# Expert stage of an attention-plus-MoE block: weight loads tied to scatter landings, gathers further ahead, deeper result buffers, one buffer for silu and product

## The chip, the cores and the metric

The kernel runs on 1 core of one Trainium2 chip. The metric is device time in microseconds (us), from start to end of one launch. Engines: TensorE (PE, with its weight loads as PEld), VectorE (DVE), ScalarE (ACT), GpSimd (POOL), and SyncE (SP), which here only issues DMAs. SP's DMAs run in queue q1, POOL's indirect DMAs in queue q0; both are carried by the same 16 DMA engines.

## What is computed

One transformer block over 2048 tokens of width 512, in float32: linear attention (16 heads of 128), then a mixture of experts. Its last part, which the change touches, is

```python
gu = jnp.einsum('ech,ehf->ecf', buf, w_gate_up)      # 32 experts, 512 -> 2 x 256
g, u = jnp.split(gu, 2, axis=-1)
act = jax.nn.silu(g) * u
y = jnp.einsum('eci,eih->ech', act, w_down)          # 256 -> 512
routed_out = jnp.einsum('tk,tkh->th', w_r, y_exp)    # weighted sum over a token's experts
```

`buf[e]` are the layer-normed rows of the tokens that chose expert e (at most 256 in two tiles of 128); each row carries its routing weights behind it, so that `act` can be multiplied by the weight before the second product. The result is added to the residual already in `out`.

## The kernel before

Attention and routing come first and fill some 730 us. Then `experts` runs 32 experts (NE), one after the other. Each needs 1 MB of up weights (two DMAs of 512 KB) and 512 KB of down weights; every float32 matrix is split into a high and a low part (ACT copies to fp32r, DVE subtracts), so each product is three rounds of matmuls.

For expert e, tile t (0 or 1; the second only for experts with enough tokens, decided at run time by `both`):

- POOL, `gather` (L1213): an indirect DMA brings the token rows into `xg[:, e % 6, t]`; six slots. From e = 6 it waits for `m_a` of expert e-5 by count, that is for the product of expert e-6, the last reader of the slot.
- PE, `turn` (L1254): transposes into PX; ACT `x_high` (L1378) and DVE `x_low` (L1324) split it.
- PE, `up` (L1268): 12 matmuls into PG. ACT `silu` (L1401) writes `s`, DVE `act` (L1331) multiplies with the other half of PG and the weight into `a[:, e % 2, t]`.
- PE, `turn_a` (L1277), ACT `a_high`, DVE `a_low`, PE `down` (L1290): 6 matmuls into PY.
- ACT, `weigh` (L1413): copies PY to `y[:, e % 4, t]`. From e = 4 it waits until the scatters of expert e-4 have landed (`m_s`, 32 counts an expert).
- POOL, `scatter` (L1223): an indirect DMA adds the rows of `y` to `out`. The first of an expert waits until all scatters of the expert before have landed, since two may hit the same row. Experts whose row count is above 64 get two scatters, the others one of 64 rows.

The order on each engine is written by hand. PE in iteration e does `turn_a(e-1)`, `turn(e+1)`, `up(e)`, `down(e-1)`; ACT and DVE split the weights of expert e+2 in iteration e, and `weigh(e-1)` is ACT's last there. POOL in iteration e gathers expert e+6 and then scatters expert e, after twelve gathers ahead of the loop.

SP loads weights into a ring of eight experts. `load e` (e from 8 on) waits for `up(e-8)` and `down(e-8)`, and also for `m_wl`, the count of low parts that DVE has made: part p of load e may start when part p of expert e-5 has been split, which DVE does in iteration e-7.

In the text, iteration e of an engine is its loop body for e; "expert k's scatter" is the one of L1223 for k. In the trace the two-scatter experts are 0, 1, 11, 15, 18, 25 and 27, and PE works two tiles for 0, 1, 11, 18, 25 and 27.

Of the kernel before, what the change touches and what calls it, by code (L numbers as in the profile page):

```python
# [5 lines left out]
P = 128  # L6
D = 512
# [5 lines left out]
NE = 32  # L13
# [8 lines left out]
ALU = mybir.AluOpType  # L22
ACT = mybir.ActivationFunctionType
# [1054 lines left out]
RING = 8  # L1078

def load_up(sm, eng, ring, wgu, e, halves=(0, 1)):
    up, _, _, _ = ring[e % RING]
    for i in halves:
        k = slice(2 * i, 2 * i + 2)
        eng.dma_start(up[:, k, :], wgu[e, k].rearrange("k p f -> p k f")).then_inc(sm[f"m_wg{e % RING}"], 16)

def load_down(sm, eng, ring, wd, e):
    _, down, _, _ = ring[e % RING]
    eng.dma_start(down, wd[e].rearrange("k p f -> p k f")).then_inc(sm[f"m_wd{e % RING}"], 16)  # L1090
# [32 lines left out]
def experts(nc, sm, wgu, wd, xn2d, out, si, ring, consts, w_h, w_l, v_h):  # L1123

    with ExitStack() as ctx:
        def sb(name, shape, dt=F32):
            return ctx.enter_context(nc.sbuf_tensor("m_" + name, shape, dt))

        def ps(name, n=512):  # L1130
            return ctx.enter_context(nc.psum_tensor("m_" + name, [P, n], F32))

        xg = sb("xg", [P, 6, 2, XW])
        xT_h = sb("xT_h", [P, 2, 2, 4, P], F32R)
        xT_l = sb("xT_l", [P, 2, 2, 4, P], F32R)
        s = sb("s", [P, 2, 256])
        a = sb("a", [P, 2, 2, 256])
        a_h = sb("a_h", [P, 2, 256], F32R)
        a_l = sb("a_l", [P, 2, 256], F32R)
        y = sb("y", [P, 4, 2, D])  # L1140
        with nc.sbuf_tensor("m_raw", [P, 2, 512], F32) as raw:
            pass
        low = sb("low", [P, 2, 512], F32R)
# [4 lines left out]
        PG = [ps("PG0"), ps("PG1")]  # L1148
        PA = [ps("PA0"), ps("PA1")]
        PY = [ps("PY0"), ps("PY1")]  # L1150
# [9 lines left out]
        def flags(eng, name):  # L1160
            return [eng.alloc_register(f"{name}{i}") for i in range(7)]
# [20 lines left out]
        with nc.Block() as block:  # L1182
            @block.sync
            def _(eng):
                eng.dma_start(ident[:, :], consts[:, 0:128]).then_inc(sm["m_id"], 16)
                eng.wait_ge(sm["m_g01"], 16)
                load_up(sm, eng, ring, wgu, 6)
                load_down(sm, eng, ring, wd, 6)
                eng.wait_ge(sm["m_g11"], 16)
                load_down(sm, eng, ring, wd, 7)  # L1190
                for e in range(RING, NE):
                    for part in range(3):
                        for t in range(2):
                            eng.wait_ge(sm[f"m_gu{t}" if part < 2 else f"m_yd{t}"], e - RING + 1)
                        eng.wait_ge(sm["m_wl"], 3 * (e - RING + 3) + part + 1)
                        if part < 2:
                            load_up(sm, eng, ring, wgu, e, (part,))
                        else:
                            load_down(sm, eng, ring, wd, e)
                eng.wait_ge(sm["m_s"], 32 * NE)  # L1200

            @block.gpsimd
            def _(eng):
                regs = flags(eng, "mp")

                def gather(e, t):

                    i = 2 * e + t
                    if e >= 6:
                        eng.wait_ge(sm[f"m_a{t}"], e - 5)  # L1210
                    else:
                        eng.wait_ge(sm["m_xg"], i + 1)
                    eng.indirect_dma_start(  # L1213
                        xg[:, e % 6, t, :], None, xn2d[:, :],
                        bass.IndirectOffsetOnAxis(ap=si[:, i:i + 1], axis=0),
                        bounds_check=T - 1, oob_is_err=False).then_inc(sm[f"m_g{t}{e % 6}"], 16)

                def scatter(e, t, rows, done):
                    i = 2 * e + t
                    if t == 0 and e >= 1:  # L1220
                        eng.wait_ge(sm["m_s"], 32 * e)
                    eng.wait_ge(sm[f"m_y{t}"], e + 1)  # L1222
                    eng.indirect_dma_start(  # L1223
                        out[:, :], bass.IndirectOffsetOnAxis(ap=si[0:rows, i:i + 1], axis=0),
                        y[0:rows, e % 4, t, :], None, compute_op=ALU.add).then_inc(sm["m_s"], done)

                for e in range(6):
                    gather(e, 0)
                    gather(e, 1)
                for e in range(NE):  # L1230
                    if e + 6 < NE:
                        gather(e + 6, 0)
                        gather(e + 6, 1)
                    if e == 0:
                        eng.wait_ge(sm["m_full"], 1)
                    load_full(eng, regs, e)
                    with eng.If_lt(regs[e % 7], T):  # L1237
                        scatter(e, 0, P, 16)
                        scatter(e, 1, P, 16)
                    with eng.Else():  # L1240
                        scatter(e, 0, 64, 32)
# [71 lines left out]
            @block.vector  # L1313
            def _(eng):
                regs = flags(eng, "mv")

                def w_low(e, parts):
                    if e < NE:
                        for part in parts:
                            split_low(sm, eng, ring, w_h, e, part)  # L1320

                def x_low(e, t):
                    eng.wait_ge(sm[f"m_xTh{t}"], e + 1)
                    eng.tensor_tensor(flat(xT_l[:, e % 2, t]), PX[t][:, :], f(flat(xT_h[:, e % 2, t])),  # L1324
                                             ALU.subtract).then_inc(sm[f"m_xTl{t}"], 1)

                def act(e, t):
                    eng.wait_ge(sm[f"m_si{t}"], e + 1)
                    if e >= 2:
                        eng.wait_ge(sm[f"m_at{t}"], e - 1)  # L1330
                    eng.scalar_tensor_tensor(out=a[:, e % 2, t, :], in0=PG[t][:, 256:512],  # L1331
                                             scalar=xg[:, e % 6, t, D + e:D + e + 1], in1=s[:, t, :],
                                             op0=ALU.mult, op1=ALU.mult).then_inc(sm[f"m_a{t}"], 1)

                def a_low(e, t):
                    eng.wait_ge(sm[f"m_ah{t}"], e + 1)
                    eng.tensor_tensor(a_l[:, t, :], PA[t][:, 0:256], f(a_h[:, t, :]), ALU.subtract).then_inc(sm[f"m_al{t}"], 1)

                def clear(e, t):
                    eng.memset(xg[:, e, t, :], 0.0).then_inc(sm["m_xg"], 1)  # L1340

                for e in range(4):
                    clear(e, 0)
                    clear(e, 1)
                load_flag(eng, regs, 0)
                both(eng, regs, 0, x_low, "m_xTl1")
                for e in range(4, 6):
                    clear(e, 0)
                    clear(e, 1)
                eng.tensor_copy(full[:, :], si[64:65, :]).then_inc(sm["m_full"], 1)  # L1350
                w_low(0, (2,))
                w_low(1, (0,))
                load_flag(eng, regs, 1)
                both(eng, regs, 0, act, "m_a1")
                w_low(1, (1,))
                both(eng, regs, 1, x_low, "m_xTl1")
                both(eng, regs, 0, a_low, "m_al1")
                w_low(1, (2,))
                w_low(2, (0, 1))
                load_flag(eng, regs, 2)  # L1360
                both(eng, regs, 2, x_low, "m_xTl1")
                w_low(2, (2,))
                both(eng, regs, 1, act, "m_a1")
                w_low(3, (0, 1, 2))
                for e in range(2, NE + 1):
                    load_flag(eng, regs, e + 1)
                    both(eng, regs, e - 1, a_low, "m_al1")
                    both(eng, regs, e + 1, x_low, "m_xTl1")
                    w_low(e + 2, (0, 1))
                    both(eng, regs, e, act, "m_a1")  # L1370
                    w_low(e + 2, (2,))

            @block.scalar
            def _(eng):
# [21 lines left out]

                def silu(e, t):
                    eng.wait_ge(sm[f"m_gu{t}"], e + 1)
                    if e >= 1:
                        eng.wait_ge(sm[f"m_a{t}"], e)  # L1400
                    eng.activation(s[:, t, :], PG[t][:, 0:256], ACT.Silu).then_inc(sm[f"m_si{t}"], 1)  # L1401

                def a_high(e, t):
                    eng.wait_ge(sm[f"m_at{t}"], e + 1)
# [3 lines left out]

                def weigh(e, t):
                    eng.wait_ge(sm[f"m_yd{t}"], e + 1)  # L1410
                    if e >= 4:
                        eng.wait_ge(sm["m_s"], 32 * (e - 3))
                    eng.activation(y[:, e % 4, t, :], PY[t][:, :], ACT.Copy).then_inc(sm[f"m_y{t}"], 1)  # L1413

                w_high(1, (0, 1))
                eng.wait_ge(sm["m_id"], 16)
# [90 lines left out]
```

## Time and profile before

| | |
|---|---|
| time, median of 3 runs | 973.87 us (973.5 to 981.56) |
| the profiled execution's time | 979.09 us |
| its span in the trace | 977.3 us |
| busy in the span: PE / DVE / ACT / POOL | 92% / 79% / 51% / 49% |
| first transpose of the expert stage | 740.1 us |
| last matmul of the expert stage ends | 962.5 us |
| last scatter starts | 969.2 us |

Times in the trace are counted from the start of the span. A row of the timeline gives start, duration, engine, line and operation, how many were merged, and in brackets the idle time before it with what ended it. A row of the windows gives busy time and count for each engine, then the granted TensorE clock (1.00 is full), the mean busy share of the 16 DMA engines and the GB/s moved.

### The profile page before, as it was taken

How to read it: one execution, taken by the hardware profiler on the slowest of the kernel's cores; microseconds unless marked ns; L12 is line 12 of the kernel's file. 1: busy time of each engine (PE TensorE's matmuls, PEld its weight loads, DVE VectorE, ACT ScalarE, POOL GpSimd, SP SyncE). 2: the span in 40 equal slices, each digit the busy share in tenths (PEclk: the TensorE clock that was granted, in tenths of full speed). 3: DMA queues.
4: the chain of work that ended last, by engine and by line, in shares of the span. 5: the costliest groups of instructions: out<-in, count | busy, mean ns of one | idle time of the engine just before them, and what ended most of it. 6: DMA issues, size and time to landing. Idle time of an engine off the chain costs nothing. (4 is left out here: it accounts for less than half of the span.)

```text
span 977.3 us, 14567 instructions
## 1 busy us (share of the span) xinstructions
PE 902.5 (92%) x4362; PEld 731.1 (75%) x4362; DVE 772.9 (79%) x1843; ACT 503.3 (51%) x867; POOL 482.5 (49%) x395
## 2 busy tenths in 40 slices
PE   4789999999999999999969999999976999998893
PEld 3577888888888888888848888888854677776672
DVE  6978888888888889888977777777776788887670
ACT  5455655555554655554563222332224687876671
POOL 2466766666766667766630000000006456775662
PEclk9999999999999999999999999999998999999897
DMA  8001111111111111110563676443155699999633
GB/s 309 6 33 49 51 46 50 59 45 49 39 59 50 44 59 51 39 59 35 195 224 145 209 266 208 148 148 119 56 192 185 162 331 323 293 299 279 201 43 43
DMA packets 67368, 127.06 MB, mean 130 GB/s; under 512 B 12072, under 2 KB 14504, under 8 KB 65232
## 3 DMA queue, kind: packets, MB, share of 16 engines
q1 hardware_dynamic: 58144, 114.67, 33.7%
q0 software_dynamic: 9136, 11.31, 6.2%
q8 instruction: 43, 0.70, 0.3%
q14 instruction: 45, 0.37, 0.1%
HBM read 106.53 MB, written 32.90 MB: 143 GB/s over the span
## 5 line engine op out<-in xcount | busy, mean ns | idle before, releaser
L595 POOL TENSOR_TENSOR a_t<-a_t 128x512 f32<-128x512 f32 x80 | 105.1, 1314 | 99.0 <-DVE a_t L358 99.0
L604 POOL TENSOR_TENSOR a_fQ<-a_fQ,a_den 128x512 f32<-128x512 f32 x64 | 88.0, 1375 | 71.8 <-DVE a_den L396 71.8
L213 PE MATMUL a_PQ<-w_h,a_xT_h 128*128 128x512 f32 x384 | 106.9, 400 | 10.1 <-DVE w_l L345 9.4
L782 PE MATMUL r_PY<-w_h,r_o_h 128*128 128x512 f32 x256 | 105.9, 414 | 3.4 <-DVE r_o_l L884 3.4
L1070 POOL TENSOR_SCALAR r_vr<-r_mv 128x1 f32<-128x1 f32 x16 | 8.4, 525 | 196.6 <-DVE r_mv L895 196.6
L213 PE MATMUL a_PQ<-w_l,a_xT_h 128*128 128x512 f32 x384 | 104.5, 395 | 0.0
L213 PE MATMUL a_PQ<-w_h,a_xT_l 128*128 128x512 f32 x384 | 103.4, 391 | 0.0
L782 PE MATMUL r_PY<-w_h,r_o_l 128*128 128x512 f32 x256 | 101.0, 395 | 0.0
L1223 POOL DMA_INDIRECT out<-m_y,si x39 | 69.1, 1772 | 64.5 <-DMA out<-m_y,si 51.2
L782 PE MATMUL r_PY<-w_l,r_o_h 128*128 128x512 f32 x256 | 100.5, 393 | 0.0
L392 DVE CUSTOM_DVE_ANT_0 a_m<-a_fQ,a_z 128x128 f32<-128x128 f32 x256 | 100.4, 445 | 0.0
L1213 POOL DMA_INDIRECT m_xg<-xn2d,si x64 | 79.0, 1235 | 39.5 <-DVE m_xg L1340 18.2
L611 POOL TENSOR_TENSOR a_A_l<-a_A,a_A_h 128x512 fp32r<-128x512 f32 x64 | 89.0, 1391 | 6.5 <-ACT a_A_h L480 6.5
L213 PEld LDWEIGHTS a_PQ<-w_h,a_xT_h 128*128 128x128 f32 x384 | 70.0, 190 | 25.3 <-issue 11.2
L357 DVE TENSOR_TENSOR a_t<-a_PQ,a_tab 128x512 f32<-128x512 f32 x80 | 55.0, 688 | 41.7 <-PE a_PQ L213 41.7
L213 PEld LDWEIGHTS a_PQ<-w_l,a_xT_h 128*128 128x128 f32 x384 | 73.2, 191 | 15.8
L494 ACT ACTIVATE a_t<-a_t 128x512 f32<-128x512 f32 x80 | 50.0, 625 | 67.4 <-POOL a_t L595 67.2
L213 PEld LDWEIGHTS a_PQ<-w_h,a_xT_l 128*128 128x128 f32 x384 | 72.9, 190 | 15.4
L480 ACT ACTIVATE a_QT_h<-a_PT 128x512 fp32r<-128x512 f32 x64 | 38.1, 596 | 80.7 <-PE a_PT L221 80.7
L1120 DVE TENSOR_TENSOR w_l<-v_l,w_h 128x1024 fp32r<-128x1024 f32 x48 | 57.2, 1222 | 5.7 <-ACT w_h L1114 4.3
L782 PEld LDWEIGHTS r_PY<-w_h,r_o_h 128*128 128x128 f32 x256 | 48.5, 189 | 12.0 <-issue 3.8
L782 PEld LDWEIGHTS r_PY<-w_h,r_o_l 128*128 128x128 f32 x256 | 48.5, 189 | 11.2
(182 smaller groups left out, 2245.3 us busy)
## 6 DMA issues: line engine op xcount, KB each, us to landing
oT<-a_o SPq DMA_DIRECT2D x64, 256.0 KB, 2.4
v_l<-in_wgu SPq DMA_DIRECT2D x32, 512.0 KB
raw<-in_wgu SPq DMA_DIRECT2D x24, 512.0 KB
v_l<-oT SPq DMA_DIRECT2D x11, 1024.0 KB, 7.2
v_l<-in_wd SPq DMA_DIRECT2D x16, 512.0 KB
raw<-in_wd SPq DMA_DIRECT2D x12, 512.0 KB
v_h<-oT SPq DMA_DIRECT2D x5, 1024.0 KB, 6.9
out<-r_x SPq DMA_DIRECT2D x18, 256.0 KB, 2.0
```

What stands on the lines that cost most here:

```text
L213: last = eng.matmul(bank[:, :], a[:, k, :], w[:, 4 * i + k, :], start=s == 0 and k == 0, stop=s == 2 and k == 3)
L357: eng.tensor_tensor(heads(t1[:, r % 2, :]), q, spread(tab[:, c % 2, 0, :]), ALU.mult)
L392: last = eng.tensor_tensor_reduce(m[:, cols], fQ[:, n % 3, cols], z[:, c % 2, g * P:(g + 1) * P], 1.0, 1e-6, ALU.mult, ALU.add, den[:, n % ...
L480: eng.activation(out, in_, ACT.Copy).then_inc(sm[kind], 1)
L494: eng.activation(t2[:, r % 2, :], t1[:, r % 2, :], ACT.Relu, scale=-1.0).then_inc(sm["r"], 1)
L595: eng.tensor_tensor(t1[:, r % 2, :], t1[:, r % 2, :], t2[:, r % 2, :], ALU.add).then_inc(sm["xr"], 1)
L604: eng.tensor_tensor(q, q, den[:, n % 2, :].unsqueeze(2).broadcast_to([P, 4, P]), ALU.mult).then_inc(sm["fs"], 1)
L611: eng.tensor_tensor(A_l[:, n % 2, :], A[:, n % 2, :], f(A_h[:, n % 2, :]), ALU.subtract).then_inc(sm["Al"], 1)
L782: last = eng.matmul(PY[c % 2][:, :], a[:, c % 2, h * P:(h + 1) * P], b[:, h, :], start=h == 0 and s == 0, stop=h == NH - 1 and s == 2)
L1120: eng.tensor_tensor(low, src, high.bitcast(F32), ALU.subtract).then_inc(sm["m_wl"], 1)
L1213: eng.indirect_dma_start(xg[:, e % 6, t, :], None, xn2d[:, :], bass.IndirectOffsetOnAxis(ap=si[:, i:i + 1], axis=0), bounds_check=T - 1, o ...
L1223: eng.indirect_dma_start(out[:, :], bass.IndirectOffsetOnAxis(ap=si[0:rows, i:i + 1], axis=0), y[0:rows, e % 4, t, :], None, compute_op=AL ...
```

## The change

Five edits, all in `experts`:

1. The load of expert e no longer waits for DVE's split; from e = 10 it waits for the landed scatters of expert e-10 (count 32(e-9)). Loads 8 and 9 wait only for `up` and `down` of experts 0 and 1.
2. POOL gathers further ahead: in its iteration e up to expert e+6 for e < 3, e+7 for e from 3, e+8 from 8. The number of slots stays six.
3. `y` becomes two buffers: six results for first tiles, four for second tiles; `weigh` waits for the scatters of expert e-6 or e-4.
4. `silu` writes into `a`, and the product overwrites it; `s` is gone. `silu` now waits for `turn_a(e-2)` where it waited for the product of e-1, and `act` loses its own wait.
5. In SBUF `y` grows from 16 to 20 KB a partition and `s` (2 KB) goes.

```diff
-        s = sb("s", [P, 2, 256])
-        y = sb("y", [P, 4, 2, D])
+        y = [sb("y0", [P, 6, D]), sb("y1", [P, 4, D])]
+        deep = (6, 4)
@@ SP
-                        eng.wait_ge(sm["m_wl"], 3 * (e - RING + 3) + part + 1)
+                        if e >= RING + 2:
+                            eng.wait_ge(sm["m_s"], 32 * (e - RING - 1))
@@ POOL, scatter
-                        y[0:rows, e % 4, t, :], None, compute_op=ALU.add).then_inc(sm["m_s"], done)
+                        y[t][0:rows, e % deep[t], :], None, compute_op=ALU.add).then_inc(sm["m_s"], done)
@@ POOL
+                asked = 6
                 for e in range(NE):
-                    if e + 6 < NE:
-                        gather(e + 6, 0)
-                        gather(e + 6, 1)
+                    ahead = e + 7 + (e >= 3) + (e >= 8)
+                    while asked < min(ahead, NE):
+                        gather(asked, 0)
+                        gather(asked, 1)
+                        asked += 1
@@ DVE, act
-                    if e >= 2:
-                        eng.wait_ge(sm[f"m_at{t}"], e - 1)
                     eng.scalar_tensor_tensor(out=a[:, e % 2, t, :], in0=PG[t][:, 256:512],
-                                             scalar=xg[:, e % 6, t, D + e:D + e + 1], in1=s[:, t, :],
+                                             scalar=xg[:, e % 6, t, D + e:D + e + 1], in1=a[:, e % 2, t, :],
@@ ACT, silu
-                    if e >= 1:
-                        eng.wait_ge(sm[f"m_a{t}"], e)
-                    eng.activation(s[:, t, :], PG[t][:, 0:256], ACT.Silu).then_inc(sm[f"m_si{t}"], 1)
+                    if e >= 2:
+                        eng.wait_ge(sm[f"m_at{t}"], e - 1)
+                    eng.activation(a[:, e % 2, t, :], PG[t][:, 0:256], ACT.Silu).then_inc(sm[f"m_si{t}"], 1)
@@ ACT, weigh
-                    if e >= 4:
-                        eng.wait_ge(sm["m_s"], 32 * (e - 3))
-                    eng.activation(y[:, e % 4, t, :], PY[t][:, :], ACT.Copy).then_inc(sm[f"m_y{t}"], 1)
+                    if e >= deep[t]:
+                        eng.wait_ge(sm["m_s"], 32 * (e - deep[t] + 1))
+                    eng.activation(y[t][:, e % deep[t], :], PY[t][:, :], ACT.Copy).then_inc(sm[f"m_y{t}"], 1)
```

## Rows read from the trace of the kernel before

**Rows 1.** Chain that ended last: start, us, what; the link through a gather
```profile
902.42 6.56 DMA m_xg<-xn2d,si
```

**Rows 2.** Groups by line, POOL, 784 to 917 us
```profile
L1213 POOL DMA_INDIRECT m_xg<-xn2d,si x38 | 49.7, 1307 | 11.6 <-issue 11.0 <-ACT m_y L1413 0.3 <-DVE m_a L1331 0.3
L1223 POOL DMA_INDIRECT out<-m_y,si x23 | 42.5, 1847 | 33.5 <-DMA out<-m_y,si 31.7 <-issue 1.2 <-ACTq L1180 0.6
```

**Rows 3.** Timeline of POOL: scatters (experts 1, 2, 3, 8, 10, 11, 15, 21, 24, 25, 30, 31)
```profile
776.33 1.57 POOL L1223 DMA_INDIRECT out<-m_y,si  x1 [0.30 <-issue]
...
784.95 1.67 POOL L1223 DMA_INDIRECT out<-m_y,si  x1 [4.12 <-DMA out<-m_y,si]
...
791.76 1.98 POOL L1223 DMA_INDIRECT out<-m_y,si  x1 [2.48 <-DMA out<-m_y,si]
...
824.06 2.29 POOL L1223 DMA_INDIRECT out<-m_y,si  x1 [0.91 <-DMA out<-m_y,si]
...
837.18 2.14 POOL L1223 DMA_INDIRECT out<-m_y,si  x1 [0.30 <-issue]
...
843.16 1.94 POOL L1223 DMA_INDIRECT out<-m_y,si  x1 [0.30 <-issue]
...
871.37 2.20 POOL L1223 DMA_INDIRECT out<-m_y,si  x1 [0.74 <-DMA out<-m_y,si]
...
916.63 1.48 POOL L1223 DMA_INDIRECT out<-m_y,si  x1 [0.30 <-issue]
...
933.31 1.93 POOL L1223 DMA_INDIRECT out<-m_y,si  x1 [0.31 <-issue]
...
938.19 2.06 POOL L1223 DMA_INDIRECT out<-m_y,si  x1 [0.31 <-issue]
...
965.34 1.44 POOL L1223 DMA_INDIRECT out<-m_y,si  x1 [2.52 <-DMA out<-m_y,si]
969.18 1.43 POOL L1223 DMA_INDIRECT out<-m_y,si  x1 [2.40 <-DMA out<-m_y,si]
```

**Rows 4.** Timeline of PE: starts of iterations 21, 22, 25; late transposes; the last matmuls
```profile
882.85 0.44 PE L1277 MATMUL m_PA<-m_ident,m_a 128*128 128x128 f32 x2 [0.94 <-DVE m_a L1331]
...
888.42 0.44 PE L1277 MATMUL m_PA<-m_ident,m_a 128*128 128x128 f32 x2
...
907.14 1.11 PE L1254 MATMUL m_PX<-m_ident,m_xg 128*128 128x128 f32 x4 [3.95 <-DMA m_xg<-xn2d,si]
...
915.26 0.38 PE L1277 MATMUL m_PA<-m_ident,m_a 128*128 128x128 f32 x2
...
961.88 0.62 PE L1290 MATMUL m_PY<-w_h,m_a_l 128*128 128x512 f32 x2
```

**Rows 5.** Timeline of SP's queue: up loads of experts 8, 12 and 31
```profile
768.41 1.50 SPq L1085 DMA_DIRECT2D raw<-in_wgu  x2
...
789.79 1.50 SPq L1085 DMA_DIRECT2D v_l<-in_wgu  x2
...
913.07 1.50 SPq L1085 DMA_DIRECT2D v_h<-in_wgu  x2
```

**Rows 6.** Windows, all engines, columns as told above
```profile
784.00:917.00 133.00, 120.82 (x549) 92.39 (x549) 106.13 (x133) 102.34 (x155) 91.04 (x61) 0.96 0.95 299
748.00:768.00 20.00, 14.20 (x61) 10.79 (x60) 11.38 (x16) 9.41 (x16) 10.77 (x9) 0.83 0.36 78
785.00:790.00 5.00, 4.77 (x23) 3.48 (x22) 4.39 (x7) 4.25 (x7) 3.67 (x3) 1.00 1.06 386
830.00:835.00 5.00, 5.00 (x27) 4.20 (x26) 4.41 (x5) 4.20 (x7) 3.57 (x2) 1.00 0.74 229
```

**Rows 7.** Windows at the start of the stage, and ACT's late silu in the timeline
```profile
747.50:750.00 2.50, 1.60 (x12) 1.12 (x10) 1.11 (x2) 0.00 (x0) 1.89 (x3) 1.00 1.05 386
...
750.00:752.50 2.50, 0.37 (x2) 0.29 (x2) 0.91 (x2) 0.38 (x1) 1.89 (x3) 0.92 0.21 55
...
751.17 0.38 ACT L1401 ACTIVATE m_s<-m_PG 128x256 f32<-128x256 f32 x1 [5.59 <-remote]
```

## Prediction

> **What bounds the kernel now.** I read the chain that ended last first, then POOL's groups by line, then the timelines of POOL, PE and SP, then windows. The chain names POOL's scatters and gathers from 897 us on, with one detour through a gather that landed late and the transposes behind it [rows 1]. So the question is how long POOL has been the limit. Its groups between 784 and 917 us add up to the stretch: gathers 49.7 + 11.6 us, scatters 42.5 + 33.5 us, together 137 us with the edges, and of the idle part 31.7 us ended when an earlier scatter landed [rows 2]. Only traces of idle time ended on a result or on a free gather slot (0.3 us each). POOL never waits for PE there; it is a chain of its own, gather, gather, scatter, wait for the landing, from expert 1's second scatter at 776.33 to expert 31's at 969.18 [rows 3].
>
> Its pace is the next thing to see. From expert 3's scatter (791.76) to expert 21's (916.63) are 124.9 us for 18 experts. Three of these (11, 15, 18) have a second scatter, which costs an issue of 1.85 + 0.3 us [rows 2], 6.5 us together, so one expert takes (124.9 - 6.5) / 18 = 6.58 us. PE's iteration takes 5.57 us (882.85 to 888.42) [rows 4]. POOL falls behind a microsecond an expert, until PE meets it: expert 25's gather, issued by 902.42, lands 6.56 us later [rows 1] and PE's transposes wait 3.95 us for it [rows 4]. Between iteration starts 888.42 and 915.26 PE takes 26.84 us for three iterations that need 3 x 5.57 + 0.4 (a second transpose tile) = 17.1, so it loses 9.8 us, part of it as slower matmuls after the idle time. That loss isn't the end's cause: even after it the end hangs on POOL, whose last scatter starts 6.7 us after the last matmul has ended (961.88 + 0.62) [rows 3, 4].
>
> Why 6.58 us? The DMA engines are 95% busy from 784 to 917 us at 299 GB/s, 386 GB/s at the best of these windows [rows 6]. Where their share fell to 0.74, at 830 to 835, the following scatters came 5.98 us apart (837.18 to 843.16), with no wait for a landing [rows 3, 6]. Once the loads are over, the distance is 4.88 us with gathers (933.31 to 938.19) and 3.84 us without (965.34 to 969.18) [rows 3].
>
> **Loads tied to landings.** Per POOL iteration the weights are the same amount: landing k releases load k+10, and before, between scatters 3 and 21, loads 13 to 31 went out too. What changes is when. Before, PE's and DVE's pace of 5.6 us pushes loads at a POOL that takes 6.58; now a load follows POOL's own landings, so the queue is less deep on average, and the idle gap after a PE stall is not followed by a crowd. Bounds for the pace: unchanged at 6.58, and 5.07 us, what POOL needs if every wait for a landing went ((133 - 31.7) / 20 experts) [rows 2]. The nearest row is 5.98 at a lighter load [rows 3]; but the new load is issued at the very moment when the next scatter is, so I don't take all of it: 6.2 us, 0.38 x 18 = **-6.8 us** (0 to -27).
>
> The first loads move too. Load 8 waited for DVE until 768.41 [rows 5]; it now starts when `up(0)` is done, about 748, and load 9's up part about 765. The DMA engines are 36% busy from 748 to 768 [rows 6], so some 1.5 to 2.5 MB leave the crowded stretch. Expert 2's scatter waited 4.12 us and expert 3's 2.48 us for landings [rows 3]; 2 MB at 386 GB/s is 5 us of DMA time. I take half of that two-step wait, **-3 us** (0 to -5).
>
> Are the later loads late? Load 31 goes out when scatter 21 has landed, about 922 at the old pace against 913.07 [rows 5], and its first reader is ACT's split in iteration 29, three iterations of 5.57 us and the last products before the end of PE's work: about 944, or 934 with PE unstalled. A load takes 1.57 MB / 299 GB/s = 5.3 us. That leaves over 6 us even then, so the price is nothing, as long as POOL's lag stays under about six iterations.
>
> **Code fetch at the start.** While loads 6 and 7 saturate DMA (share 1.05 to 750 us), ACT stands for 5.59 us for something outside its program and resumes at 751.17, just as the share drops to 0.21 [rows 7]. Load 8's 1.05 MB now comes right behind and prolongs the crowd by 1.05 / 386 = 2.7 us. If ACT's fetch sits behind it, PE and with it POOL's first scatters come that much later; 0 to +2.7, I take **+1.5 us**. By that rule the price would be the full 2.7 and the sum 1.2 us worse; the trace agrees that the wait ends with the crowd, but shows no second case.
>
> **Gathers further ahead.** Same 64 gathers. In POOL's iterations 3 and 8 four are issued instead of two: 2 x (1.31 + 0.3) = 3.2 us each [rows 2], of which the waits for a landing there hid 2.48 and 0.91 [rows 3]: +0.7 and +2.3. Iterations 24 and 25 lose theirs: at most 4.88 - 3.84 = 1.04 us for each [rows 3], together I take -1.6. Net **+1.4 us** (-1 to +5). The gather of expert e+8 must wait for the product of expert e+2, with scatter e queued behind it on POOL. POOL works expert 21's scatter at 916.63, when PE is in iteration 25: the product is there. Around experts 9 to 11 the lead is near two iterations and it may cost 1 us, inside that bound. On PE's side the two iterations of lead (11 us) cover the 6.56 us of a late gather: the 9.8 us stall goes. It isn't in the sum, since the end hangs on POOL; it says what PE would allow.
>
> **Six results.** `weigh` waits for scatter e-6 where it was e-4. It only matters where POOL is more than four iterations behind, which is so where scatter 21 starts at 916.63 with PE already in its iteration 25 (915.26) [rows 3, 4]; it removes the same stall as the gathers, again off POOL's chain: 0. Second tiles keep four; experts 18, 25, 27 need scatters 14, 21, 23, landed before by the pace above.
>
> **Silu and product in one buffer.** Same instructions and sizes; the new wait (a transpose of two experts ago) is long over when `up` ends, DVE has one instruction less: 0 to -1 us over 32 experts, on PE and so covered.
>
> **Sum.** -6.8 - 3 + 1.5 + 1.4 = -6.9 us on the profiled execution: 979.1 - 6.9 = 972.2. That execution was 5.2 us over the median of 973.87; by the median it would be 967.0. Its stalls and POOL's lag seem part of that difference, so most of the effect should be there in a median run: **968 us**.
>
> **Rivals.**
> - *PE becomes the limit.* If POOL's pace falls to about 5.9, the chain no longer binds. PE ends 9.8 us sooner, and the last scatter starts 1 us behind it instead of 6.7: -15.5, so 958.4 by the median and 963.6 by the profile, 961. For: POOL's waits hold 31.7 us. Against: POOL's issues alone went to 5.98 us where no landing was waited for. Chance 0.22.
> - *POOL's pace stays.* Equal bytes between equal scatters, equal landing time. Then only the small terms are left, about 0: 973 to 976. For: DMA share 0.95. The Trainium skill, "DMA: Bandwidth & Descriptors", section "Queues, rings and completion order", says that each DMA engine takes turns between queue rows packet by packet; by that a deep load queue would not hold a scatter back more than a shallow one, and pacing loads gives nothing. Expert 15's scatter at 871.37 had waited only 0.74 us for a landing in the loaded stretch [rows 3], which fits it in part; expert 2's 4.12 us doesn't. Chance 0.23.
> - *Slower: the burst meets the scatter.* Each landing releases 1.5 MB of loads and the next scatter at once. If that makes every landing as slow as the worst rows (784.95 to 791.76, 6.8 us; 7.1 with a little more), POOL takes +0.4 to 0.5 us an expert, +8 over 18, and the extra gathers come on top: 980 to 984. It decides from a pace of 6.7 us. Chance 0.15.
> - *As forecast*, pace 6.0 to 6.4: 963 to 972. Chance 0.40.
>
> About 1% (9.7 us) is what a measurement of this kernel can tell from no change. Faster by more (under 964.1) takes the first rival and a small part of the forecast: 0.30. Slower by more (over 983.6) only the top of the third: 0.10. The rest, 0.60, is the same. The range reaches from the first rival's 959 to 979, leaving out its best part and most of the slower case.
>
> **What would show it.** Right: scatters 3 to 21 about 6.2 us apart with less wait on `out` landings; no PE wait for `m_xg`; load 8 issued about 748 and load 31 after scatter 21; the last scatter 2 to 5 us behind the last matmul. Wrong: the same 6.6 us (second rival), ACT waits on weights, POOL idle behind a product (L1331), or ACT's silu at the start later than 752.

## The result, and the profile after

The change made the kernel slower: 997.3 us against 977.6 us before (medians of 4 runs each; the first three runs of before are those shown above, and the fourth moved its median up from 973.87), a ratio of 1.0252 with a 95% interval of 1.021 to 1.0293. The profiled execution took 997.3 us, its span 995.5 against 977.3, which is 18.2 us more. The forecast was 968, the range 959 to 979.

The stretch is where the forecast looked for a gain, only with the other sign. POOL's timeline, as in [rows 3] (scatters of experts 3, 12, 13, 21, 22, 23 and 31; start, duration, in brackets the idle time before):

```profile
790.43 1.47 POOL L1224 DMA_INDIRECT out<-m_y,si  x1 [0.81 <-DMA out<-m_y,si]
...
861.67 1.48 POOL L1224 DMA_INDIRECT out<-m_y,si  x1 [3.79 <-DMA out<-m_y,si]
...
868.95 2.17 POOL L1224 DMA_INDIRECT out<-m_y,si  x1 [2.40 <-DMA out<-m_y,si]
...
931.95 1.47 POOL L1224 DMA_INDIRECT out<-m_y,si  x1 [2.71 <-DMA out<-m_y,si]
...
938.95 1.47 POOL L1224 DMA_INDIRECT out<-m_y,si  x1 [2.88 <-DMA out<-m_y,si]
...
947.45 1.47 POOL L1224 DMA_INDIRECT out<-m_y,si  x1 [3.92 <-DMA out<-m_y,si]
...
987.43 1.42 POOL L1224 DMA_INDIRECT out<-m_y,si  x1 [2.58 <-DMA out<-m_y,si]
```

Three pieces make up the 18.2 us. Expert 3's scatter starts at 790.43 (before 791.76): -1.3. From expert 3 to 21 it is 141.5 us (before 124.9): +16.6. From 21 to 31 it is 55.5 us (before 52.6): +2.9. By the prediction's own count the pace between 3 and 21 is (141.5 - 6.5) / 18 = 7.50 us an expert, where it was 6.58 and 6.2 was expected. The +2.9 belong to the same thing: scatters 22 and 23 are 8.50 us apart (before 4.95), and load 31, the last, went out 0.2 us ahead of scatter 22.

POOL's groups by line over that stretch (790 to 932 us), to be held beside [rows 2]:

```profile
L1214 POOL DMA_INDIRECT m_xg<-xn2d,si x38 | 47.4, 1246 | 11.6 <-issue 10.7 <-DVE m_a L1333 0.3 <-ACT m_y L1415 0.3
L1224 POOL DMA_INDIRECT out<-m_y,si x22 | 39.7, 1804 | 45.2 <-DMA out<-m_y,si 42.2 <-DVE m_a L1333 2.1 <-issue 0.6
```

POOL's own work an instruction is the same or less (1246 and 1804 ns; before 1307 and 1847). What grew is the wait for the landing of the scatter before: 42.2 / 22 = 1.92 us a scatter, before 31.7 / 23 = 1.38. The windows of the changed kernel show that this isn't because the DMA engines are busier:

```profile
784.00:917.00 133.00, 120.95 (x558) 92.31 (x559) 106.60 (x133) 102.49 (x154) 81.64 (x58) 0.97 0.82 246
```

In the same 133 us the DMA engines are busy 82% at 246 GB/s, before 95% at 299 [rows 6]. Landings got slower while less was moved. The timeline of SP's queue points at the reason, which the experiments then test (loads of expert 22 here: up, then down):

```profile
861.47 0.88 SPq L1085 DMA_DIRECT2D v_l<-in_wgu  x2
862.46 0.41 SPq L1090 DMA_DIRECT2D v_l<-in_wd  x1
```

The up loads are issued at 861.47 and scatter 12 starts at 861.67: load and scatter are let go by the same landing, and SP is the quicker by 0.2 us, at nearly every turn. The DMA issues of 784 to 932 us say how they then land (size, median us from issue to landing):

```profile
v_l<-in_wgu SPq DMA_DIRECT2D x21, 512.0 KB, 4.1
...
v_l<-in_wd SPq DMA_DIRECT2D x11, 512.0 KB, 6.3
...
out<-m_y,si POOLq DMA_INDIRECT x23, 7.2
```

The scatter lands 7.2 us after its start, though it moves 128 KB and the loads 1.5 MB. The up loads, issued 0.2 us ahead of it, have landed before it does. The down load, issued some 0.8 us behind the scatter's start, lands at about the same time as the scatter: 0.8 + 6.3 = 7.1 us.

### The profile page after: what moved, and what is told of

It is laid out like the page before. It is cut to its first block and busy times, and to the rows that moved or that the text cites. A ratio compares the mean times of both kernels' runs of the same rounds, so it can differ in the third digit from the quotient of the medians.

```text
span 995.5 us, 14529 instructions
## 1 busy us (share of the span) xinstructions
PE 906.2 (91%) x4362; PEld 732.2 (74%) x4362; DVE 772.2 (78%) x1843; ACT 503.5 (51%) x867; POOL 479.0 (48%) x395
## 5 line engine op out<-in xcount | busy, mean ns | idle before, releaser
L1214 POOL DMA_INDIRECT m_xg<-xn2d,si x64 | 76.3, 1192 | 37.5 <-DVE m_xg L1342 17.7
```

What stands on the lines that cost most here:

```text
L1214: eng.indirect_dma_start(xg[:, e % 6, t, :], None, xn2d[:, :], bass.IndirectOffsetOnAxis(ap=si[:, i:i + 1], axis=0), bounds_check=T - 1, o ...
```

## The experiments

All ratios are to the kernel before, run on the same chip beside them. "Pace" is counted as above, from expert 3's scatter to expert 21's.

**Which edit it is.** Two runs, one with the load release put back and one with it alone:

```diff
                         for t in range(2):
                             eng.wait_ge(sm[f"m_gu{t}" if part < 2 else f"m_yd{t}"], e - RING + 1)
-                        if e >= RING + 2:
-                            eng.wait_ge(sm["m_s"], 32 * (e - RING - 1))
+                        eng.wait_ge(sm["m_wl"], 3 * (e - RING + 3) + part + 1)
```

> The changed kernel with one edit undone: load e waits again for DVE's split of expert e-5 instead of the landed scatters of expert e-10. Theory A (the landing release lengthens every landing): the pace from expert 3's to expert 21's scatter goes from 7.5 us an expert back to about 6.6, DMA share from 0.83 to about 0.95, and the time to 973 to 981, at or a little below the kernel before. Rival B (four extra early gathers and waits for products or for second-tile results cost the time): pace stays above 7.2 us and the time stays at 990 or more.

975.7 us, ratio 1.0013 (0.998 to 1.0047), pace 6.75 us. The other four edits together change nothing that can be measured.

The reverse of that diff in the kernel before:

> The kernel before with only the load release changed to landings of expert e-10. Theory A: pace 7.4 to 7.6 us an expert, time 993 to 1003; with only four result buffers and gathers six ahead PE stalls as well, but the end hangs on POOL, so it is no slower than that. Rival B: the pace stays at about 6.6 us and the time within 1% of 977.

999.0 us, ratio 1.0232 (1.0208 to 1.0256), pace 7.70 us, a little over the 7.4 to 7.6 expected. The release alone is the whole loss. With six gathers ahead and four results PE now waits 21.5 us for gathered rows and ACT 30.4 us for landings, and the end is within half a percent of the changed kernel's: those waits are not on the chain that ends last.

The gathers alone, in the kernel before:

```diff
+                asked = 6
                 for e in range(NE):
-                    if e + 6 < NE:
-                        gather(e + 6, 0)
-                        gather(e + 6, 1)
+                    ahead = e + 7 + (e >= 3) + (e >= 8)
+                    while asked < min(ahead, NE):
+                        gather(asked, 0)
+                        gather(asked, 1)
+                        asked += 1
```

> The kernel before with only the gathers further ahead (up to eight, six slots). Theory A: POOL's chain is nearly the same, PE's waits for gathers go, time within 1% of before (970 to 981). Rival B: the extra gathers ahead of scatters 3 and 8 and the waits for products slow POOL's chain, 985 or more.

974.8 us, ratio 0.9994 (0.9972 to 1.0016), pace 6.71 us. PE's waits for gathered rows fall from 8.0 to 0.8 us and the time does not move.

**Is a throttle needed at all?** The changed kernel without the two lines of the landing release:

> The changed kernel with no throttle on the loads: load e waits only for the products of expert e-8 that read its slot. If holding loads back from POOL's transfers were what sets the pace, the crowd would be greater and the time 985 or more. If the landing release alone is the loss, the loads run at PE's pace, about a microsecond an expert faster: pace 6.4 to 6.9, time 968 to 980.

976.8 us, ratio 1.0022 (0.9987 to 1.0057), pace 6.76 us. With the old throttle (1.0013) or with none (1.0022) the time is the same; tying the loads to the landing is what costs. That takes away my reason for the gain: a deeper load queue costs nothing here. A less deep one was only ever tried tied to the landing.

**Lump or moment?** The landing release differs from the old one in two ways: all 1.5 MB go out back to back, and always at the start of a scatter. The kernel before with only the lump:

```diff
-                        eng.wait_ge(sm["m_wl"], 3 * (e - RING + 3) + part + 1)
+                        eng.wait_ge(sm["m_wl"], 3 * (e - RING + 3) + 3)
```

> The kernel before with its release by DVE's split, but all three loads of expert e wait for the last part of expert e-5, so that they go out back to back as in the changed kernel, at PE's pace and not at the landings. Theory A1-lump (1.5 MB at once is what hurts): pace 7.0 to 7.5, time 983 to 995. Theory A1-phase (it hurts only where it always meets the start of a scatter): within 1% of before, 970 to 982.

981.6 us, ratio 1.0036 (0.9999 to 1.0074); the profiled execution, at 984.6 us one of the slower ones, has a pace of 6.93. The lump costs at most a third of the loss (0.7% by the top of the interval, of 2.5%).

**The moment, first try (failed as a test).** A count that POOL raises behind each scatter was to let the loads go 2 us later:

```diff
-                            eng.wait_ge(sm["m_s"], 32 * (e - RING - 1))
+                            eng.wait_ge(sm["m_iss"], e - RING)
@@ POOL, last in the loop body
+                    eng.sem_inc(sm["m_iss"], 1)
```

> The changed kernel with the load of expert e released when POOL has issued the scatter of expert e-9, which is the one that was waiting for the landing of e-10: the same pace of release, but 1.5 to 2.5 us later, behind the scatter in time instead of ahead of it. Theory A1 (the loads get into the DMA engines ahead of the scatter, which then has to pass through them): landings come 2 us or more sooner, pace 6.0 to 6.6, time 970 to 982. Theory A2 (any load within one POOL iteration costs the landing the same): pace 7.3 to 7.7, time 992 to 1002.

995.9 us, ratio 1.0214 (1.0191 to 1.0237), pace 7.46 us. By the time alone this would have favoured "any load costs the same". The timelines say otherwise. POOL:

```profile
866.67 1.83 POOL L1224 DMA_INDIRECT out<-m_y,si  x1 [2.73 <-DMA out<-m_y,si]
...
873.68 1.47 POOL L1224 DMA_INDIRECT out<-m_y,si  x1 [1.56 <-DMA out<-m_y,si]
```

and SP's queue of the same kernel:

```profile
866.53 1.54 SPq L1085 DMA_DIRECT2D v_l<-in_wgu  x2
...
873.85 0.88 SPq L1085 DMA_DIRECT2D v_h<-in_wgu  x2
```

The loads go out 0.14 us before and 0.17 us after the scatter's start: the count was up when the scatter in front of it had only begun on POOL, not when it had ended there 1.5 to 1.8 us later. The loads were hardly moved, so the run decides nothing between the theories, but it is a good base for the next one.

**The moment, second try.** A small DMA of 8 KB on SP's queue, whose landing SP awaits, ahead of the down load in one kernel and, with `part == 0`, ahead of all three in the other:

```diff
                         if e >= RING + 2:
                             eng.wait_ge(sm["m_s"], 32 * (e - RING - 1))
+                        if e >= RING + 2 and part == 2:
+                            eng.dma_start(dly[:, :], consts[:, 0:16]).then_inc(sm["m_dly"], 16)
+                            eng.wait_ge(sm["m_dly"], 16 * (e - RING - 1))
```

> The changed kernel with, from expert 10, an 8 KB DMA into a scratch tile issued between the up loads and the down load; SP waits for its landing before it issues the down load. The up loads still go out with the landing, the down load 2.5 to 5 us later. Theory A1 (it is the lump of 1.5 MB at one moment that the scatter issued then has to pass): pace from 7.5 to 6.6 to 7.0 us an expert, time 978 to 987. Theory A3 (each load follows a landing and each landing follows a load, so one expert costs the sum of both whatever the order): pace 7.3 to 8, time 992 to 1010.

993.5 us, ratio 1.0181 (1.0134 to 1.0227), pace 6.98 us.

> The changed kernel with, from expert 10, the same small DMA and wait ahead of the up loads: all three loads go out 2.5 us or more after the landing, when POOL has already made the next scatter's descriptors. Theory A1 (what counts is that the loads are ahead of the scatter): pace 6.0 to 6.7, time 970 to 980. Theory A3: the small DMA's time doesn't matter to the scatter or is added to it, pace 7.2 to 8, time 990 to 1010.

993.5 us, ratio 1.0183 (1.0122 to 1.0245), pace 6.94 us. Both times are as Theory A3 gave them, and both paces below what it gave. The delay was not the 2.5 us planned. SP's queue in the second kernel:

```profile
867.37 0.39 SPq L1199 DMA_DIRECT2D m_dly<-in_cr  x1
873.73 0.88 SPq L1085 DMA_DIRECT2D v_l<-in_wgu  x2
```

The 8 KB follow their predecessor's 1.5 MB in the same queue, and the next load goes out 6.4 us after them (median of 22: 6.1 us, from 3.3 to 9.0), so each load waits for the one before to land, and the loads come too late. The first kernel's waits show it (ACT, us in total, times, longest):

```profile
ACT w_h L1114 <- DMA v_l<-in_wd: 16.8, 8, 4.3
```

In these kernels the lost time has a second cause, so their time is no verdict. But in the second kernel the loads, no longer held to the landing, slide past the scatters, and its two timelines give the distance of scatter k to k+1 by where the nearest up loads were issued (turns with two scatters or four gathers left out; 14 turns between experts 4 and 21):

```
up loads from 3.6 to 1.5 us ahead of the scatter's start:  4.67  5.21  6.68  6.17     mean 5.68 us
within 1.4 us of it, ahead or behind:  7.61 6.59 7.06 8.89 6.83 8.71 6.80 8.08        mean 7.57 us
1.9 to 3.6 us behind it:                                   5.27  4.42                 mean 4.85 us
```

That is within one execution of one kernel, and there is no memset in it. The turns of the first kernel, sorted the same way, give 7.4 us (8 turns within 1.5 us) against 6.2 us (6 turns outside). These numbers were the ground for the next run.

**The moment, third try.** The count of the first try, raised now by POOL's engine with a small memset (of a column of a scratch tile) behind the scatter:

```diff
-                    eng.sem_inc(sm["m_iss"], 1)
+                    eng.memset(mark[:, e:e + 1], 0.0).then_inc(sm["m_iss"], 1)
```

> As the run that was to release the loads behind the next scatter, but now with a count that POOL's engine raises by a small memset behind the scatter of expert e-9, so that the loads go out about 1.8 us after that scatter's start. In the run with the small DMA ahead of all loads, scatters with loads 1.8 to 3 us behind their start or over 3 us ahead of it came 4.4 to 5.7 us apart, those with loads within 1.5 us of it 6.2 to 8.9. Theory A1 (the moment relative to the scatter counts): pace 5.4 to 6.2 us an expert, time 955 to 968. Theory A3 (a load in each expert's turn costs the landing the same): pace 7.2 to 7.8, time 990 to 1000.

976.3 us, ratio 0.9958 (0.9924 to 0.9992), pace 6.31 us. The same release by the same count as in the first try, 1.8 us later (loads 1.68 us behind the scatter's start in the median, there 0.14 ahead): from 2.1% slower than before to 0.4% faster. The memset itself costs POOL nothing: it runs under the scatter, ends 0.1 us behind it, and the next gather starts 0.30 us after the scatter's end (863.65 + 1.48 to 865.43), as without it. POOL's timeline:

```profile
863.65 1.48 POOL L1225 DMA_INDIRECT out<-m_y,si  x1 [0.30 <-issue]
864.61 0.63 POOL L1247 MEMSET m_mark<- 128x1 f32 x1
865.43 1.34 POOL L1215 DMA_INDIRECT m_xg<-xn2d,si  x1 [0.19 <-issue]
...
869.13 1.47 POOL L1225 DMA_INDIRECT out<-m_y,si  x1 [1.05 <-DMA out<-m_y,si]
```

and SP's loads beside it:

```profile
865.33 0.88 SPq L1085 DMA_DIRECT2D v_l<-in_wgu  x2
866.32 0.42 SPq L1090 DMA_DIRECT2D v_l<-in_wd  x1
```

The loads start 1.68 us behind scatter 13, and the next scatter comes 5.48 us after it; in the changed kernel the same two were 7.29 us apart (868.95 to 876.24). POOL's groups from expert 3 to 21:

```profile
L1215 POOL DMA_INDIRECT m_xg<-xn2d,si x38 | 50.9, 1340 | 13.6 <-issue 8.7 <-DVE m_a L1335 5.0
L1225 POOL DMA_INDIRECT out<-m_y,si x21 | 35.8, 1706 | 17.0 <-DMA out<-m_y,si 13.1 <-issue 3.4 <-ACTq L1181 0.6
L1247 POOL MEMSET m_mark<- 128x1 f32 x18 | 11.4, 633 | 0.0
```

13.1 us of waits for landings for 21 scatters, 0.62 us each, against 1.92 in the changed kernel. And the DMA engines are busier than there, with a share of 0.95 against 0.82 (windows of the same kernel):

```profile
797.00:917.00 120.00, 114.91 (x538) 88.29 (x538) 101.70 (x127) 97.94 (x148) 88.78 (x77) 1.00 0.95 284
```

The pace, at 6.31, misses the 5.4 to 6.2 that I expected, and the time, at 976, misses 955 to 968. Part of both is 5.0 us of gathers that now wait for products (POOL is near its lead of two experts), 0.3 us an expert. Part of the time lies ahead of this stretch: expert 3's scatter starts at 797.24, before 791.76, see below. The profiled execution was the slowest of the ten (979.3 us).

**One expert earlier**, with the same place within the turn:

```diff
-                            eng.wait_ge(sm["m_iss"], e - RING)
+                            eng.wait_ge(sm["m_iss"], e - RING - 1)
```

> The same with the release one expert earlier: load e behind the issue of expert e-10's scatter. Theory A1: the same pace of 5.4 to 6.2 and the same time as with e-9, 955 to 968, since only the place within the turn counts. If the lead of the loads were what counts, it is faster or slower than the run with e-9 by over 0.5%.

974.8 us, ratio 0.9958 (0.9925 to 0.9992), pace 6.07 us: the same ratio, and again not the 955 to 968. Whether a load comes an expert earlier doesn't count, where it falls in the turn does. In this kernel expert 1's scatter starts only at 777 us (changed kernel: 772.1). ACT's timeline at the start of the stage:

```profile
751.82 0.38 ACT L1405 ACTIVATE m_a<-m_PG 128x256 f32<-128x256 f32 x1 [4.99 <-remote]
755.39 0.60 ACT L1382 ACTIVATE m_xT_h<-m_PX 128x512 fp32r<-128x512 f32 x1 [3.19 <-remote]
```

and the windows of the same kernel, while it stands:

```profile
754.00:756.00 2.00, 0.00 (x0) 0.00 (x0) 0.00 (x0) 0.60 (x1) 0.73 (x1) 0.50 1.04 403
```

This is the wait that I had taken for a code fetch and priced at 0 to 2.7 us. Its second part, 3.19 us, meets load 8, issued at 751.87; the kernel with the later release stood 3.90 us there. The kernel before had this second wait too, with no load beside it:

```profile
753.34 1.32 ACT L1378 ACTIVATE m_xT_h<-m_PX 128x512 fp32r<-128x512 f32 x2 [1.79 <-remote]
```

So beside load 8 it is 1.4 to 2.1 us longer. That the wait is for code is my reading: the profile says only that something outside ACT's program ended it.

**Loads 8 and 9 late again**, on top of that kernel:

```diff
                             eng.wait_ge(sm["m_iss"], e - RING - 1)
+                        else:
+                            eng.wait_ge(sm["m_wl"], 3 * (e - RING + 3) + part + 1)
```

> The kernel of the last run (loads released by the count behind the issue of scatter e-10) with loads 8 and 9 waiting for DVE's split as in the kernel before. In the last run load 8 filled the DMA engines from 754 to 756 us while ACT stood 3.19 us for its code, and expert 1's scatter started at 777 instead of 772 to 774. If that is the cost of the early first loads: expert 1's scatter at 773 to 775 and the time 2 to 5 us below the last run, 970 to 973, a ratio of 0.988 to 0.994 to before. If the early first loads pay by emptying the stretch from 768 us: 975 to 980, since the pace up to expert 8 gets slower.

968.5 us, ratio 0.994 (0.9913 to 0.9967); expert 1's scatter at 773, pace 6.26 us. It is faster than the kernel before, by 0.6% only. Its median is lower than the last run's by more than its ratio tells, since the kernel before ran 0.7% faster beside it as well. ACT's waits are not in this profile at all, so what load 8 cost is not settled by this pair, and whether there is a gain over the run before neither: the ratios, 0.994 and 0.9958, overlap in their intervals.

**Gathers six ahead again**, on top:

> The same, with POOL's gathers six ahead as in the kernel before. The turns with four gathers took 8.4 and 7.3 us where their neighbours took 5.9. If they are a net cost to POOL's chain: 1 to 3 us less than the last, 968 to 971. If PE needs the longer lead, its waits for gathered rows come back (over 3 us in the loaded stretch), but the end stays on POOL: within 1 us.

970.7 us, ratio 0.9943 (0.9919 to 0.9966), pace 6.11 us; PE waits 4.1 us for gathered rows. No difference can be measured, for or against the extra lead of the gathers.

The turns of all kernels with the old release or none (before, the one with the release put back, the one with the gathers alone, the lumped one, the one without a throttle) can be sorted the same way (experts 4 to 21, as long as loads still go out): with up loads within 1.5 us of the scatter's start the mean distance is 6.7 us (26 turns), otherwise 6.2 (39 turns). There the effect is weak. A reason may be that a load's parts are spread (before, a down load goes out 2.3 us or more behind its up loads) and that loads of other turns are still under way; this was not tested. In the three kernels with release at the landing all 42 turns lie within 0.5 us, mean 7.45 us; in the four with the memset all 56 lie over 1.5 us behind, mean 6.08 us.

## Why the prediction was wrong, point by point

**What bounds the kernel: right.** POOL's chain carried the end before and after. The best evidence is what didn't matter: PE's waits for gathers removed, 0.9994; PE's and ACT's long waits with only the release changed, no slower than the whole change.

**Loads tied to landings, the pace (-6.8 us): this is the step that failed.** It came out at +16.6, and +2.9 more in the turn of load 31. I wrote in the same paragraph that "the new load is issued at the very moment when the next scatter is", and used that only to take less of a gain. The DMA engines did get less busy (0.95 to 0.82), but the landings got slower.

I had taken the distance of 5.98 us as a sign that a lighter load makes landings faster, and that row was misread. The share of 0.74 is that of 830 to 835 us; the turn of 5.98 us runs from 837.18 to 843.16, and the windows of the kernel before give for it:

```profile
835.00:840.00 5.00, 4.53 (x20) 3.21 (x19) 4.37 (x6) 4.60 (x7) 4.09 (x4) 1.00 0.98 278
840.00:845.00 5.00, 4.88 (x23) 3.72 (x22) 4.30 (x6) 4.20 (x6) 4.39 (x3) 1.00 0.99 325
```

So one of the quicker turns fell on DMA engines that were full, and the "nearest row" said nothing for a lighter load. Share was the wrong variable: the changed kernel has a share of 0.82 and a pace of 7.50, the kernel before 0.95 and 6.58, the one with the memset 0.95 and 6.31. A bound of "unchanged at 6.58" on the bad side had no reason behind it either; the trace of before held turns of 6.8 to 7.5 us, and nothing said that they would not become the rule. (The other bound, 5.07, counts the second scatters in, which 6.58 leaves out; by the same count it is 4.74.)

**The rival "the burst meets the scatter": the right mechanism, priced too low.** It had +0.4 to 0.5 us an expert from the worst rows I named; measured +0.92. I gave it a chance of 0.15. The worst turn of before was not among those rows: expert 5's, 804.23 to 811.69, is 7.46 us and would have given +0.9. And the price should have come from the moment that the rival describes, all three loads within 1 us of the start of nearly every scatter, which no turn of before had (there a down load follows its up loads by 2.3 us or more), so its worst rows were no upper bound.

**The first loads early (-3 us): not borne out.** Counted from the first gather of the stage, expert 3's scatter comes after 52.4 us in the changed kernel (738.05 to 790.43) and after 55.6 before (736.16 to 791.76), which is -3.2 us and looks like the forecast. But it is 52.2 us in the kernel with the old release and its late first loads, and 52.1 in the one without a throttle, which differs from it in that wait alone and has the first loads early. In this pair the early loads gave 0.1 us. The -3.2 go with the wait of ACT at the start of the stage, which the kernel before had and these three don't. That the number came near was luck.

**Later loads not late: right in time, with thin margins.** ACT waited 2.2 us in all for weights.

**Code fetch (+1.5 us): not in this profile; about right where the wait was there.** ACT's wait of 5.59 us [rows 7] is gone in the changed kernel, with nothing in its place, and back in the two kernels with a memset and an early load 8. The Trainium skill's "Runtime: NRT & Kernel Launch" ("Instruction fetch mechanics") has a taken branch whose target is outside the current window cost a fetch by DMA. No run here shows that this wait is such a fetch, nor what makes it come and go; each kernel was traced once. With load 8 beside it, ACT's second wait is 3.90 and 3.19 us against 1.79 before, which is 1.4 to 2.1 us more.

**Gathers ahead (+1.4 us): nothing that can be measured.** With the gathers alone the ratio was 0.9994 (0.9972 to 1.0016, about 2 us either way). The two turns behind which the four gathers lie say no more: expert 2 to 3 and 7 to 8 took 8.2 and 8.6 us in that kernel (before 6.8 and 6.3, expected +0.7 and +2.3), but 8.2 and 7.1 us in the last pair of runs with them and 8.2 and 6.6 without.

**Six results (0 us): right for the end, wrong in part of its reason.** I counted on scatters 21 and 23 landing "by the pace above". At 7.5 us they didn't, and the four buffers of the second tile held ACT up:

```profile
938.76 0.60 ACT L1415 ACTIVATE m_y<-m_PY 128x512 f32<-128x512 f32 x1 [11.70 <-DMA out<-m_y,si]
```

PE stood 6.14 us behind it (matmuls of 940.20). The end did not get later by it, but only just: the result of expert 25's second tile was written at 958.32, and POOL itself was ready for its scatter at 958.31. The stall was not tried alone.

**Silu in the product's buffer (0 to -1 us):** within the 1.0013 of the run with the release put back; not separable.

**The rival "POOL's pace stays"** rested on "DMA: Bandwidth & Descriptors" of the Trainium skill ("Queues, rings and completion order"): engines take turns between queue rows by packet. Two runs agree with what I drew from it for a deep queue: the time is the same with the old throttle (1.0013) and without any (1.0022). Drawn further, it would let 128 KB be done well before the 1.5 MB that were let go beside them, and that the trace does not show: the scatter lands behind both up loads and at about the time of the down load.

## What to carry to other kernels

When two transfers are let go by the same event, they meet in every turn; a mean over a trace in which they met now and then does not price that. Before tying a large load to a semaphore that also starts a small transfer on the critical chain, put the load behind the small one's issue: 1.8 us of shift took the ratio from 1.021 to 0.996 here. It won little over loads that are tied to nothing (1.002), so the point is above all what not to tie together. And a resource that is partly free on the average (DMA share 0.82) says nothing about the latency at the moment that counts.

## What the runs showed of the hardware that I had not expected

- A scatter-add of 64 rows lands 7.2 us after its start (median) when the first of 1.5 MB of loads are issued 0.2 us ahead of it. The scatters then come 7.45 us apart, and 6.08 us apart when the loads start 1.7 us or more behind. What in the DMA engines makes 1.8 us count that much was not found; only the dependence is shown.
- A semaphore increment that follows an indirect DMA in POOL's program takes effect about when that DMA starts on POOL (most loads 0.14 us ahead to 0.17 us behind the scatter's start); the increment of a memset put there comes 1.8 us later (loads 1.66 us or more behind the start).
- An 8 KB DMA on a queue whose predecessors move 1.5 MB was seen as landed after 6.1 us in the median (3.3 to 9.0 us).
- ACT's wait at the start of the stage for something outside its program came and went between kernels with the same ACT program: none in the profile of the changed kernel, 4.99 + 3.19 us in that of one that differs only in what POOL and SP do.
